# The copy of the spread reciprocals placed ahead of the projection copies in ScalarE's slot

## The reference, cut to what matters

```
q = (x @ Wq + bq).reshape(B, S, H, D)      # k and v likewise
q = _apply_rope(q, cos, sin)
k = _apply_rope(k, cos, sin)
scores = einsum('bshd,bthd->bhst', q, k) / sqrt(D)     # causal mask above the diagonal
attn = softmax(scores, axis=-1)
out = einsum('bhst,bthd->bshd', attn, v).reshape(B, S, E)
return out @ Wo + bo
```

## Time and profile before

| | |
|---|---|
| median of 3 runs | 987.56 us (985.23 to 988.04) |
| the profiled execution's own time | 983.27 us |
| its span, first to last instruction | 981.5 us |
| PE busy | 931.8 us (95%) |
| DVE busy | 728.4 us (74%) |
| POOL busy | 597.2 us (61%) |
| ACT busy | 514.0 us (52%) |
| mean granted TensorE clock | 0.996 of full speed |
| chain that ended last | PE 71%, DVE 9%, ACT 8%, POOL 5%, issue 4%, DMA 2% |

### The profile page before, as it was taken

One profiled execution on the slowest core, in us unless ns is written; L12 is line 12 of the kernel. 1 busy time (PEld: TensorE's weight loads), 2 busy tenths in 40 slices (PEclk: granted clock), 3 DMA queues, 4 the chain that ended last, 5 costly groups with the idle time before them and its releaser, 6 DMA issues.

```text
span 981.5 us, 16194 instructions
## 1 busy us (share of the span) xinstructions
PE 931.8 (95%) x5272; PEld 754.7 (77%) x5272; DVE 728.4 (74%) x1588; ACT 514.0 (52%) x1150; POOL 597.2 (61%) x645
## 2 busy tenths in 40 slices
PE   7787999999999987998999999999999999999997
PEld 5565877777778765887878888888778878888885
DVE  5566778768877877688777767777777877767767
ACT  4576777767777777557244443333533253333333
POOL 2465745844765646456567775667846776665644
PEclk9999999999999999999999999999999999999998
DMA  6875665966676691002102011111111033011002
GB/s 226 245 197 152 194 161 152 259 158 174 164 203 183 173 280 43 22 38 114 65 0 65 33 65 65 33 65 65 32 34 65 33 108 108 33 65 65 33 33 86
DMA packets 40739, 105.20 MB, mean 107 GB/s; under 512 B 4944, under 2 KB 5072, under 8 KB 38608
## 3 DMA queue, kind: packets, MB, share of 16 engines
q1 hardware_dynamic: 40656, 104.16, 36.0%
HBM read 78.98 MB, written 25.17 MB: 106 GB/s over the span
## 4 chain that ended last, share of the span: by engine, by line
PE 71%; DVE 9%; ACT 8%; POOL 5%; issue 4%; DMA 2%; SPq 1%; POOLq 0%; DVEq 0%; ACTq 0%
PE pd L708 26%; PE pj L656 13%; PE pj L708 9%; PE pg L708 5%; PE pu L708 5%; PE pv L699 4%; PE ps L671 3%; PE pb L684 2%; PE pa L684 2%; ACT prob L898 1%; DVE prob L1161 1%; ACT e L942 1%; ACT raw L888 1%; ACT pT L905 1%; PE ps L656 1%
## 5 line engine op out<-in xcount | busy, mean ns | idle before, releaser
L898 ACT ACTIVATE prob<-prob,nmax 128x512 f32<-128x512 f32 (+3 forms) x256 | 144.0, 563 | 82.0 <-DVE nmax L1161 80.2
L1161 DVE CUSTOM_DVE_ANT_0 prob<-ps,mask 128x512 f32<-128x512 f32 (+3 forms) x256 | 124.6, 489 | 84.0 <-PE ps L671 77.8
L671 PE MATMUL ps<-ks,qs 128*128 128x256 f32 (+2 forms) x256 | 104.6, 410 | 8.1 <-DVE nmax L1161 6.1
L1623 POOL TENSOR_TENSOR g_lo<-gated,g_hi 128x512 fp32r<-128x512 f32 x32 | 49.5, 1546 | 94.3 <-ACT g_hi L1002 94.3
L1456 POOL TENSOR_TENSOR raw<-raw,cos 128x512 f32<-128x512 f32 x32 | 42.3, 1321 | 94.2 <-DVE pj L1143 78.8
L1294 DVE TENSOR_TENSOR xb<-pd,xb 128x512 f32<-128x512 f32 x116 | 79.4, 685 | 26.8 <-PE pd L708 26.7
L1616 POOL TENSOR_TENSOR wop_lo<-wsum,wop_hi 128x512 fp32r<-128x512 f32 x64 | 81.5, 1295 | 1.4 <-ACT wop_hi L987 1.4
L1002 ACT CAST g_hi<-gated 128x512 fp32r<-128x512 f32 x32 | 19.9, 622 | 112.1 <-DVE gated L1354 112.1
L708 PE MATMUL pd<-dn_hi,g_hi 128*128 128x512 f32 x244 | 75.4, 390 | 2.4 <-POOL g_lo L1623 1.1
L708 PE MATMUL pd<-dn_hi,g_lo 128*128 128x512 f32 x244 | 75.2, 389 | 0.0
L708 PE MATMUL pd<-dn_lo,g_hi 128*128 128x512 f32 x244 | 75.1, 389 | 0.0
(11 more groups left out here) (525 smaller groups left out, 2816.7 us busy)
## 6 DMA issues: line engine op xcount, KB each, us to landing
f_raw<-in_w_ffn SPq DMA_DIRECT2D x32, 768.0 KB, 4.2
qs<-qk_scratch SPq DMA_DIRECT2D x64, 256.0 KB, 4.6
ks<-qk_scratch SPq DMA_DIRECT2D x60, 256.0 KB, 7.1
qk_scratch<-qk_hi SPq DMA_DIRECT2D x32, 256.0 KB, 2.0
qk_scratch<-raw SPq DMA_DIRECT2D x32, 256.0 KB, 2.1
res<-in_x SPq DMA_DIRECT2D x4, 1024.0 KB, 4.9
x_scratch<-res SPq DMA_DIRECT2D x4, 1024.0 KB, 5.6
xb<-x_scratch SPq DMA_DIRECT2D x4, 1024.0 KB, 5.9
```

Source lines behind the costliest of these rows:

```text
L671: pe.matmul(ps[:, t % 2, 0:w], qs[n % 2][:, r, s * P:(s + 1) * P], ks[n % 2][:, r, 0:w], start=True, stop=True).then_inc(s_done, 1)
L898: act.activation(prob[:, t % PROBS, 0:w], prob[:, t % PROBS, 0:w], ACT.Exp, bias=nmax[:, n % 2, i:i + 1], scale=-1.0, accum_out=rsum[:, n ...
L1161: dve.tensor_tensor_reduce(prob[:, t % PROBS, 0:w], ps[:, t % 2, 0:w], mask[:, S - w:S], -D ** -0.5, 3e38, ALU.add, ALU.min, accum_out=nma ...
L1623: pool.tensor_tensor(lo, (gated, gated_b)[b][:], hi.bitcast(F32), ALU.subtract).then_inc((glo_done, glo_b_done)[b], 1)
```

## The change

`move_r` is tested for ahead of the projection copies in ScalarE's loop, in a loop of its own over the groups. Nothing else differs; every copy, wait and signal is there as before.

```
             if t % ST == 1 and 0 <= t - 5 < SCORES:
                 move_a((t - 5) // ST)
+            for n in range(GROUPS):
+                if t == hop(("r", n), 0):
+                    move_r(n)
             for key, start, counts, _ in UNITS:
                 if key[0] in "qkv" and t == ENDS[key]:
                     project(key)
@@
                 for u in range(2):
                     if t == ENDS["qk"[u], n] + SPLIT_QK:
                         split_qk(n, u)
-                if t == hop(("r", n), 0):
-                    move_r(n)
             for n in range(B * ST):
                 if t == hop(("o", n), 3):
                     layer_norm(n)
```

## The result

| | before | changed |
|---|---|---|
| median of 6 runs each, us | 985.15 (983.98 to 988.04) | 980.30 (977.46 to 980.94) |
| ratio | | 0.9942, 95% interval 0.9926 to 0.9957 |
| profiled execution: time, span, us | 983.27, 981.5 | 980.25, 978.5 |
| PV product (L699, 56 matmuls) of group 1, start, us | 85.93 | 86.69 |
| the same of group 13 | 348.77 | 344.30 |

The changed kernel is faster, by 0.58% (0.43 to 0.74%), which is 5.7 us (4.2 to 7.3) of 985.15. The forecast was 983.1 us; 980.30 lies 2.8 us under it, 0.1 us inside the lower end of the range (980.2). The level from which the forecast was taken is the larger part of this: 987.56 was the median of three runs, and with more runs the kernel before stands at 985.15, later at 984.74 (22 runs) and 984.78 (17 runs).

The account below looks back on a forecast made before the run. TensorE's own work was taken to set the pace, so its weight-load waits count. Ten groups by 0.45 us and three by 0 make 4.5 us, taken off the median: 983.1 us, range 980.2 to 987.3.

Parts of the forecast that it names:

- From there VectorE runs without a pause: After the q swap in slot 22, VectorE was taken to have no gap, so its work runs 0.17 us later.
- the 0 for the split groups: Groups 0, 4 and 8, which split the next batch's x, were each forecast to gain 0 us.
- The stall and its worth: Slot 22: TensorE's weight load for k waits for ScalarE's copy of the spread reciprocals; a stall costs 0.52 us.
- The swap itself: ScalarE's 13 copy pairs change places, taking 1.03 us either way; the q copy ends 0.46 us later, VectorE's swap 0.17.
- The slack in slots 27 and 31: Emptying of bank pa: 0.80 us slack against 0.69 needed, then 0.32; TensorE gains 0.45 us, 0.07 stays as a wait.
- Groups 0, 4 and 8: TensorE idles away its gain in slot 35, behind a chain through GpSimd's x splits whose head moves about 0.04 us earlier.
- The starting level: The 4.5 us were taken off the median of the runs shown, the profiled execution being 4.3 us under it.
- (a): Slots 22 to 31: VectorE and ScalarE absorb more; a group gains 0.12 us, 986.4 us in all; chance 0.20.
- (b): The later q copy delays whole chains to slot 31 and the x splits: 4.2 us slower, 991.8 us; chance 0.06.
- (c): TensorE's clock falls after longer idling in groups 4 and 8, taking 3.4 us of the gain: 986.5 us; chance 0.04.
- (d): All 13 groups gain, 6 to 7 us, about 981.1 us; chance 0.10.

## Why the prediction was wrong in size, and what of it was right

The step that failed is the last of the sum: "I take the same 4.5 us off the median: 983.1 us". The median of three, 987.56, was 2.4 us above the 985.15 that six runs give, and the median was taken in preference to the profiled execution. Taken off 985.15, the same 4.5 us give 980.65, 0.35 us from what was measured. The gain itself was mis-sized by less: 4.5 us against 5.2 in the groups' lengths. There the steps that failed are "From there VectorE runs without a pause", which put each plain group at 0.45 us where 0.52 was measured, and the 0 for the split groups; group 11 went the other way. That 980.30 still lies within the range is luck in part: its lower end allows for every group gaining the whole stall, and three of the 12 measured groups do not.

**The stall and its worth: right.** The waits for `heads` went, and a plain group is 0.50 to 0.52 us shorter, the 0.52 that the comparison of the two slots gave. The copy made later, the wait 0.70 longer and the group 0.72 longer, shows the same one for one.

**The swap itself: right.** The pair takes the same time; q's swap came 0.20 us later, against 0.17.

**The slack in slots 27 and 31: mis-sized, in the good direction.** The forecast let both chains run on by 0.17 us, and left 0.07 us per group in slot 31. It took VectorE to run without a pause behind the swap of q and again behind the swap of k. The timeline before shows no idle bracket there, but it has a pause all the same:

```profile
202.12 0.68 DVE L1149 TENSOR_TENSOR swp<-pj,sin 128x512 f32<-128x512 f32 x1
...
202.38 0.42 PE L671 MATMUL ps<-ks,qs 128*128 128x384 f32 x1
...
202.84 0.56 DVE L1161 CUSTOM_DVE_ANT_0 prob<-ps,mask 128x384 f32<-128x384 f32 x1
```

The maximum of slot 25 starts 0.72 us after the multiplication; in the changed kernel, where nothing holds it, 0.60 (200.79 to 201.39). It waited for the score product, which ends at 202.80. With that product 0.52 us earlier the pause takes up 0.12 of the 0.20, and the maximum is only 0.09 us later against the start of the pair (3.01 us behind it, 2.92 before). From there, all against the start of the pair, before and after: maximum of slot 27 5.35 and 4.89, swap of k 6.04 and 5.79 (0.25 earlier, forecast 0.13), copy out of `pa` for slot 31 9.14 and 8.81 (0.33 earlier, forecast 0.13). The k copy is only 0.07 later (5.01 and 5.08) where 0.17 was forecast, which makes the swap of k 0.10 earlier than forecast; and behind it stands a second hidden pause, the maximum of slot 28 starting 0.67 us after the swap of k before (205.96 to 206.63; the score product for it ends at 206.60) and 0.60 in the changed kernel (204.17, 204.77). The 0.33 and the slack of 0.32 together are more than 0.52, so nothing is left behind: 0.52 for 0.45 in nine groups, 0.6 us in all. Slot 27 had 0.33 us between copy and load, 0.21 of slack where 0.11 was forecast.

**Groups 0, 4 and 8: mis-sized.** The head of the chain, ScalarE's rounding of q, is 0.18 us earlier instead of 0.04 (in group 4 11.03 us behind the PV product, 161.06 less 150.03, and 11.21 before, 162.07 less 150.86), and groups 4 and 8 gain 0.19 each. The wait grew to 1.57, not 1.75. That GpSimd's splits hold these groups was right, and moving them showed it. Group 0 can't be measured here: the stretch to group 1 varies by 2 us between executions.

**Group 11: overlooked.** It was counted with the plain ones at 0.45 and gave 0.17, since the two casts of the context, 0.61 and 1.05 us, make ScalarE late for slot 35; moved three slots on, they gave the rest back. The sign was in the trace before: its wait of 0.33 us in slot 35, at 323.78, which no plain group has. With TensorE 0.52 us earlier it had to grow unless the chain moved; it grew by 0.34, to 0.67.

**Sum.** Forecast 10 by 0.45, 4.5 us. Measured in groups 1 to 13: 9 by 0.52, 0.17, and 2 by 0.19, 5.2 us.

**The starting level: the larger part of the miss.** Of the 2.8 us between 983.1 and 980.3, the 2.4 of the starting level are by far the most. The profiled execution's 983.27 was under all three runs shown, and the forecast set it aside; among the 22 later runs, 982.31 to 986.38, it is an ordinary one. It should have been counted as a fourth run, and the start set lower. Against 985.15 the forecast's 983.1 is a change of 2.05 us, where 4.85 was measured between the medians.

**The rivals.** (a) and (b) fell, with about 0.3 us to spare, as the later q copy showed. (c) fell: the clock is 1.00 where groups 4 and 8 idle, 1.57 us each. (d) was nearer than its chance of 0.10 said: all 12 measured groups gained something, 5.2 us together, but three of them a third of the stall or so, groups 4 and 8 by the chain that the forecast named and group 11 by the casts, which is not (d).

## What to carry to other kernels

When two copies meet in one slot of an in-order engine, put the one that a full engine waits for first, and ask of the other how late it may be; here 0.46 us cost nothing in the plain groups, since the engine behind it had unseen pauses, and a further slot of lateness cost more than the swap gives. Measure such a change by the distance between two marks inside the loop, which repeated to 0.1 us in most groups, while whole times of the same kernel lay 4 to 6 us apart; and take the level to which a forecast is applied from more than three runs, when they differ by more than half of what is forecast. And look for the group that doesn't gain: what holds it is the next thing to move, here for about as much again.

## What the runs showed of the hardware

A pause on an engine can be there with no idle shown: back to back, the multiplication and the maximum lie 0.60 us apart (200.79, 201.39), with the wait 0.72, and the timeline shows no bracket in either case, since the first instruction lasts 0.68 and 0.69 us and the next may start before it ends.

The granted clock after TensorE's short pauses isn't the same from one execution of a program to the next. In one stretch (366 to 400 us), in which TensorE is busy some 28 of 34 us and its longest pause is 1.51 us, it stayed at 1.00 in some and fell in others with pauses of the same lengths, and the way from group 14 to 15 took 24.13, 24.15, 25.08 and 27.05 us in four executions of the same kernel.
